# Operand rows of two softmax layers loaded straight from SBUF, eight places per feature, with a reordered opening

## The chip, the cores and the metric

One core of one Trainium2 chip runs the whole kernel. The metric is the device time of one execution in microseconds (us), the median of several runs; lower is better.

## What is computed

Four transformer layers on x of shape 2 x 1024 x 128 (two batches of 1024 tokens, 128 features). Each layer normalises x, shifts and scales it by values made from a small conditioning vector (the modulation), runs an attention and a feed-forward half, and adds each result back through a gate. The change touches the attention halves of layers 0 and 1, and the modulation.

```python
# layer 0: differential attention, 32 score heads of 4 features, 16 value heads of 8
q, k, v = x @ Wq.T, x @ Wk.T, x @ Wv.T          # each 1024 x 128 per batch
w = softmax(q_h @ k_h.T * 4**-0.5)              # full 1024 x 1024 for each head
attn = (w[2i] - lam * w[2i+1]) @ v_i            # then RMS norm per head, @ Wo.T
# layer 1: plain attention, 16 heads of 8 features, with biases and a key mask
w = softmax(q_h @ k_h.T * 8**-0.5 + mask)       # then @ v_h, @ Wo.T + bo
```

Layers 2 and 3 (causal latent attention with experts; linear attention) and the feed-forward halves of all layers are not touched.

## The kernel before

Arrays lie with features on partitions and the 2 x 1024 tokens along the free dimension, in four chunks of 512 tokens (`NC = 4`; chunks 0 and 1 are batch 0). Each stage is a small program for each of the five engines; the engines run their own programs in order and meet at semaphores.

**Opening.** `setup_stage` issues on SP the loads of the conditioning vector, x of batch 0, the identity, x of batch 1 and layer 0's modulation weights; `Norm.on_sp` the loads of the layer's weights. `first_norm` runs the layer norm: `centre(c)` subtracts the mean on PE, ACT squares, `variance(c)` averages on PE, ACT takes Ln and Exp, and DVE's `apply(c)` writes the chunk of `R.h`. The modulation products (12 matmuls of two columns) come after all four chunks on PE, and DVE finishes the modulation (seven short instructions) and then applies chunks 0 to 3.

**Projection** (`project_stage`). For each of eight tiles n (four chunks, query and key) PE projects, ACT rounds the result to bf16 (part 1, L561 or L559), DVE subtracts to get the rest (L608 or L605), ACT rounds that (part 2, L566), DVE subtracts again (part 3, L613). Three bf16 parts carry an f32 operand. SP stores the parts of each chunk to a DRAM tensor `parts_dram`. The value projections go between on PE, and DVE copies them to `A.v` (L627, L624). In layer 0 PE then makes the modulation products of layers 1 to 3 (36 small matmuls, L211).

**Operand rows.** Layer 0 works in 8 pairs of groups, 16 groups of 4 heads; layer 1 in 8 groups. The scores of a head are one bf16 matmul that contracts over 32 rows (layer 0) or 64 rows (layer 1): six products of query and key parts per feature, three rows for the running maximum, in layer 1 one for the mask. `load_rows` fills these rows from DRAM, per head with three transfers for the query and three for the key (L415): 24 transfers for a group of layer 0, 28 for one of layer 1 with the mask. The first group is spread over SP, ACT and POOL. `init_operands` presets the rows on POOL by memsets (L444).

**Softmax** (`softmax_stage`). One unit is a group and half of the queries. First pass: PE makes scores two banks at a time (L836), DVE takes the maximum of each pair (L966), 16 such slots for a unit; DVE joins them, POOL splits the maxima into three bf16 parts (`split`), PE turns them (`turn`, L845), DVE adds them to the query rows (`merge`, L981). Second pass: PE makes scores (L856), ACT takes Exp (L944), PE multiplies by the values (L870). Slots of the first pass of the next unit are put in between by a written order. At the start the 16 slots of unit 0 and some of unit 1 stand alone, with nothing of the second pass beside them.

**Layer 0's end.** DVE combines two maps per chunk (L1016, order 0, 1, 3, 2) with a factor that `lambda_programs` has made in the projection stage; POOL squares them (L815); PE sums the squares (L1078) once all four are there, and only then, in PE's order, comes `last_products`, the last product with the values.

```python
        pe.wait_ge(A.map_squared, 4)
        for c in range(3):
            last = pe.matmul(R.ps[32 * c:32 * c + 32, MS[0], :], W.head_sum[:], sq[:, c, :], ...)
        last.then_inc(ms, 1)
        A.last_products()
```

## Time and profile before

| | us |
|---|---|
| median of 3 runs | 2267.89 (2263.37 to 2268.41) |
| the profiled execution, its own time | 2265.14 |
| its span, first to last instruction | 2263.4 |
| TensorE busy | 2077.2 (92%) |
| VectorE busy | 1595.7 (71%) |
| ScalarE busy | 1358.9 (60%) |
| GpSimd busy | 216.5 (10%) |

The span is laid along a time axis that begins with the first instruction. Layer 0's projection begins at 22.75 us, its first maximum at 48.20 us; layer 1's projection at 742.45 us, its first maximum at 768.43 us. Busy time is an average over stages with different limits, so the windows and the timeline of the stages concerned are read, not the totals. PEclk is the granted TensorE clock as a share of full speed (1.00 is 2.4 GHz, 0.50 is 1.2 GHz).

### The profile page before, as it was taken

What the parts mean: (1) busy time and instruction counts of PE and PEld (TensorE: products, weight loads), DVE (VectorE), ACT (ScalarE), POOL (GpSimd) and SP (SyncE); (2) the same over time, 40 slices, a digit from 0 to 9 for tenths busy, and PEclk for the clock granted to TensorE, in tenths of its full rate; (3) what the DMA queues carried; (4) which work ended last, traced back from release to release, by engine and by line L of the source; (5) the groups of instructions that cost most, each with busy time, mean ns of one, the idle gap of its engine ahead of it and who ended that gap; (6) DMA issues with size and microseconds to landing.
All of it is one profiled execution on the core that took longest, in us unless ns stands there. A gap on an engine that the chain in (4) does not pass through costs nothing. (4 is left out here: it accounts for less than half of the span.)

```text
span 2263.4 us, 40899 instructions
## 1 busy us (share of the span) xinstructions
PE 2077.2 (92%) x15918; PEld 918.9 (41%) x15918; DVE 1595.7 (71%) x2012; ACT 1358.9 (60%) x2699; POOL 216.5 (10%) x397
## 2 busy tenths in 40 slices
PE   5899999999999599999889999999998989999998
PEld 3222222222224222222246566656665434444453
DVE  5999999999964899999455555555555265555553
ACT  3699999999994289999744444444445232222243
POOL 3011111111114301111000000000000010000000
PEclk7799999999999699999999999999999999999999
DMA  4000000000010200010100101010101125555520
GB/s 136 14 16 24 27 22 22 25 26 22 21 28 0 99 16 25 23 40 8 27 4 11 24 14 24 11 23 14 20 10 20 26 61 118 124 118 123 119 63 19
DMA packets 109887, 88.74 MB, mean 39 GB/s; under 512 B 51797, under 2 KB 92629, under 8 KB 105744
## 3 DMA queue, kind: packets, MB, share of 16 engines
q1 hardware_dynamic: 107700, 84.74, 15.4%
q8 instruction: 122, 2.00, 0.4%
q10 hardware_dynamic: 668, 1.04, 0.1%
q0 software_dynamic: 1344, 0.52, 0.1%
q14 instruction: 53, 0.43, 0.1%
HBM read 75.63 MB, written 8.73 MB: 37 GB/s over the span
## 5 line engine op out<-in xcount | busy, mean ns | idle before, releaser
L944 ACT ACTIVATE a0p<-ps 128x512 f32<-128x512 f32 x1024 | 544.3, 599 | 88.2 <-PE ps L856 71.4
L966 DVE TENSOR_REDUCE a0nm<-ps 128x2 f32<-128x1024 f32 x512 | 586.1, 1212 | 12.9 <-PE ps L836 10.7
L870 PE MATMUL ps<-a0p,a0vst 128*32 128x256 f32 x4096 | 328.4, 392 | 27.6 <-ACT a0p L944 14.0
L944 ACT ACTIVATE a1p<-ps 128x512 f32<-128x512 f32 x512 | 275.4, 596 | 58.3 <-PE ps L856 49.8
L966 DVE TENSOR_REDUCE a1nm<-ps 128x2 f32<-128x1024 f32 x256 | 294.5, 1214 | 12.2 <-PE ps L836 11.4
L856 PE MATMUL ps<-a0qm,a0k 32*128 32x512 bf16 x1024 | 276.7, 387 | 0.0
L1783 DVE TENSOR_REDUCE canm<-ps 128x1 f32<-128x128 f32 (+7 forms) x256 | 182.0, 752 | 115.2 <-PE ps L1646 114.6
L1734 ACT ACTIVATE cap_long<-ps,canm 128x1024 f32<-128x1024 f32 (+3 forms) x128 | 121.6, 953 | 190.1 <-DVE canm L1783 190.1
L836 PE MATMUL ps<-a0k,a0q 32*128 32x512 bf16 x1024 | 203.8, 396 | 29.1 <-DVE a0nm L966 21.8
L2015 ACT ACTIVATE ex_s<-ps 128x512 f32<-128x512 f32 x128 | 76.4, 597 | 252.9 <-PE ps L1970 252.9
L836 PE MATMUL ps<-a1k,a1q 64*128 64x512 bf16 x512 | 150.6, 405 | 26.6 <-DMA a1k<-a1mask 14.7
L870 PE MATMUL ps<-a1p,a1vst 128*32 128x256 f32 x2048 | 164.5, 393 | 6.6 <-ACT a1p L944 5.7
L2104 DVE TENSOR_TENSOR ex_su<-ex_s,ps 128x512 f32<-128x512 f32 x128 | 88.0, 688 | 116.2 <-PE ps L1974 115.9
L856 PEld LDWEIGHTS ps<-a0qm,a0k 32*128 32x128 bf16 x1024 | 79.1, 91 | 208.8 <-ACT a0p L944 119.6
L1646 PE MATMUL ps<-cak,caq 64*128 64x512 f32 (+3 forms) x768 | 158.6, 517 | 0.0
L856 PE MATMUL ps<-a1qm,a1k 64*128 64x512 bf16 x512 | 156.8, 386 | 0.0
L1659 PE MATMUL ps<-ident_res,cap_long 128*128 128x128 f32 x832 | 123.2, 281 | 29.1 <-ACT cap_long L1734 18.8
L870 PEld LDWEIGHTS ps<-a0p,a0vst 128*32 128x32 f32 x4096 | 81.6, 108 | 156.0 <-ACT a0p L944 70.7
L1970 PE MATMUL ps<-h_res,f2wg 128*128 128x512 f32 x256 | 130.7, 592 | 0.0
L1974 PE MATMUL ps<-h_res,f2wu 128*128 128x512 f32 x256 | 130.7, 592 | 0.0
L1958 PE MATMUL ps<-ex_hid,f2wd 128*128 128x512 f32 x256 | 130.5, 592 | 0.0
L1659 PEld LDWEIGHTS ps<-ident_res,cap_long 128*128 128x128 f32 x832 | 89.0, 140 | 86.0 <-issue 39.2
(305 smaller groups left out, 2515.1 us busy)
## 6 DMA issues: line engine op xcount, KB each, us to landing
ex_wb<-ex_w_dram SPq DMA_DIRECT2D x62, 512.0 KB, 6.2
carrow<-car_dram SPq DMA_DIRECT2D x32, 256.0 KB, 4.3
xc_res<-a0rec SPq DMA_DIRECT2D x15, 256.0 KB
a0parts<-a0parts_sb SPq DMA_DIRECT2D x8, 384.0 KB, 3.6
a1parts<-a1parts_sb SPq DMA_DIRECT2D x8, 384.0 KB, 3.8
f2wg<-in_ex_gate SPq DMA_DIRECT2D x32, 64.0 KB, 1.8
f2wu<-in_ex_up SPq DMA_DIRECT2D x32, 64.0 KB, 1.9
f2wd<-in_ex_down SPq DMA_DIRECT2D x32, 64.0 KB, 1.9
```

The source lines that it names most:

```text
L836: pe.matmul(R.ps[:, bank + d, :], q[rows, slot, rt, t0:t0 + 128], k[rows, slot, rt, hf * CW:(hf + 1) * CW], start=True, stop=True).then_in ...
L856: pe.matmul(R.ps[:, score_bank(n), :], k[rows, place(u)[3], rt, s * 128:(s + 1) * 128], qm[rows, u % 2, rt, :], start=True, stop=True).the ...
L870: last = pe.matmul(R.ps[32 * j:32 * j + 32, 6, cols], vst[:, g, s, j * HG // 4, :], p[:, s % 2, j, cols], start=(g == 0 and s == 0 and hal ...
L944: act.activation(p[:, s % 2, e, :], R.ps[:, score_bank(n), :], ACT.Exp).then_inc(exp_done, 1)
L966: dve.tensor_reduce(nm[:, u % 2, tb, 2 - 2 * z:4 - 2 * z, hf], R.ps[:, bank:bank + 2, :], X_AXIS, ALU.max, negate=True).then_inc(bank_free, 1)
L1646: last = pe.matmul(R.ps[:, 2 * hh + c, 0:cols], q[rows, hp % 2, b, tb * 128:(tb + 1) * 128], k[rows, hp % 2, b, c * CW:c * CW + cols], sta ...
L1659: last = pe.transpose(R.ps[:, bank, to:to + 128], p[long][:, hh, s * 128:(s + 1) * 128], R.ident[:])
L1734: act.activation(p[long][:, hh, 0:(tb + 1) * 128], src, ACT.Exp, bias=nm[:, a % 4:a % 4 + 1], accum_out=rs[:, b, tb, hh:hh + 1]).then_inc( ...
L1783: dve.tensor_reduce(nm[:, a % 4:a % 4 + 1], src, X_AXIS, ALU.max, negate=True).then_inc(max_done, 1)
L1958: pe.matmul(R.ps[:, i % 4, :], wd[:, (i // 4) % 2, :], hid[:, i % 4, :], start=False, stop=True, skip_group_check=True).then_inc(d_done, 1)
L1970: pe.matmul(R.ps[:, G_BANK + 2 * (i % 2), :], wg[:, slot, :], h_chunk(R, c), start=True, stop=True)\
L1974: pe.matmul(R.ps[:, U_BANK + 2 * (i % 2), :], wu[:, slot, :], h_chunk(R, c), start=True, stop=True)\
```

## The change

Parts stay in SBUF. Every feature has eight rows ("places") in a group's operand tile: place 0 for the mask, 1 to 6 for the six products, 7 of the first three features for the maximum. A transfer takes 16 features of one part of one operand, from 16 neighbouring partitions to 16 partitions at a stride of eight: 12 transfers for a group of layer 0, 24 and 2 for the mask in layer 1. The stores to DRAM are gone. `init_operands` needs fewer memsets.

In the projection only the parts of batch 0 (tiles 0 to 3) are made ahead of the maxima; values and the tiles of chunk 2 are projected too. The tiles of chunk 3 are projected by PE after slots 1 and 3 of unit 0, ACT makes parts 1 and 2 of batch 1, and POOL, not DVE, does the two subtractions (eight instructions of 128x512), ahead of its `split(0)`. The first group's loads are on SP in layer 0, and on SP (query, mask), POOL and ACT (key) in layer 1.

The opening of layer 0 is reordered: identity and x first, the modulation products after the first variance, DVE applies chunks 0 to 2 and, in the projection stage, chunk 3. The modulation of layers 1 to 3 goes from the projection stage into the last unit of layer 0's softmax (six shares on PE, the seven DVE instructions ahead of chunk 3 among the combined maps), with the factor lambda ahead of the maps.

```diff
@@ setup_stage
-    loads = [cT, x[0], ident, x[1], L0_wmod]
+    loads = [ident, x[0], cT, L0_wmod, x[1]]
@@ first_norm
-        for c in range(NC):
-            norm.centre(pe, c)
-            ...
-        modulation[0](pe)
+        norm.centre(pe, 0)
+        norm.centre(pe, 1)
+        pe.wait_ge(R.setup_sems.ones_done, 3)
+        norm.variance(pe, 0)
+        products(pe)
+        norm.centre(pe, 2)
+        norm.variance(pe, 1)
+        norm.variance(pe, 2)
+        pe.wait_ge(step, 1)
+        norm.centre(pe, 3)
+        norm.variance(pe, 3)
@@ load_rows
+PART_OF = ((0, 0, 0, 1, 1, 2), (0, 1, 2, 0, 1, 0))
+    for part in parts:
+        for i in range(6):
+            if PART_OF[operand][i] == part:
+                for rt in range(A.row_tiles):
+                    f = first + rt * rows
+                    queue.dma_start(dst[1 + i:122 + i:8, slot, rt, :], A.parts[f:f + rows, operand, part, b, :])\
+                         .then_inc(loaded or A.ld[slot], 16)
@@ project_stage, on_sp
-        for c in range(NC):
-            ...
-                sp.dma_start(A.parts_dram[o, :, b * C:(b + 1) * C, t].rearrange("s f t -> f s t"),
-                             parts[:, o, :, b, t]).then_inc(stored[b], 16)
+        sp.wait_ge(A.inited[0], A.n_inited[0])
+        for part in range(3):
             for o in range(2):
+                if bias and o == 1:
+                    continue
+                part_waits(sp, part, o)
+                load_rows(A, 0, 0, o, sp, (part,))
@@ project_stage, on_pool and its second parts
+            pool.wait_ge(part3, 4)
             init_operands(A, 1)(pool)
+    def second_parts(pool):
+        for n in range(4, 9):
+            if n < 8:
+                ...
+                pool.wait_ge(part1, n + 1)
+                pool.tensor_tensor(full[:, n - 4, :], full[:, n - 4, :], parts[:, o, 0, b, t], ALU.subtract).then_inc(taken, 1)
+            if n > 4:
+                ...
+                pool.wait_ge(part2, n)
+                pool.tensor_tensor(parts[:, o, 2, b, t], full[:, n - 5, :], parts[:, o, 1, b, t], ALU.subtract).then_inc(third, 1)
@@ project_stage, on_pe
+        first_batch(0)
+        first_batch(1)
+        second_batch(2, 0)
+        second_batch(2, 1)
+        for c in range(NC):
             values(c)
+        A.among_maxima = {1: lambda: second_batch(3, 0), 3: lambda: second_batch(3, 1)}
@@ project_stage, on_act (after the parts of tiles 0 to 3)
+        if bias:
+            act.wait_ge(A.inited[0], A.n_inited[0])
+            for part in (1, 2):
+                part_waits(act, part, 1)
+                load_rows(A, 0, 0, 1, act, (part,))
+        for c in (2, 3):
+            if not bias:
+                copy_values(c)
+            for o in range(2):
+                first_part(2 * c + o)
+        for n in range(4, 8):
+            act.wait_ge(taken, n - 3)
+            second_part(n, full[:, n - 4, :])
@@ project_stage, on_dve (after the parts of tiles 0 to 3)
+        if last_chunk:
+            last_chunk.apply(dve, 3)
+        copy_values(0)
+        copy_values(1)
+        if bias:
+            copy_values(2)
+            copy_values(3)
+            key_mask(1)
@@ softmax_stage, on_pool
-        pool.wait_ge(*A.v_done)
         stage_v(0)
+        A.second_parts(pool)
         split(0)
@@ softmax_stage, on_pe
-        pe.wait_ge(*A.rested)
-        if A.modulated:
-            pe.wait_ge(A.modulated, 1)
         for i in range(16):
+            if i < 2:
+                pe.wait_ge(A.v_done[i], 8)
             p1_slot(0, i)
+            if i in A.among_maxima:
+                A.among_maxima[i]()
...
+                if A.modulation and u == UNITS - 1 and 0 < s < 7:
+                    A.modulation[0](pe, s - 1, 6)
@@ softmax_stage, on_dve
         if A.maps:
+            lambda_programs(W)[2](dve)
             for c, rows in COMBINED:
+                if c == 3:
+                    A.modulation[1](dve)
```

## Rows read from the trace of the kernel before

**Rows 1.** The page, costliest groups: busy, mean ns | idle before, releaser.
```profile
L944 ACT ACTIVATE a0p<-ps 128x512 f32<-128x512 f32 x1024 | 544.3, 599 | 88.2 <-PE ps L856 71.4
L966 DVE TENSOR_REDUCE a0nm<-ps 128x2 f32<-128x1024 f32 x512 | 586.1, 1212 | 12.9 <-PE ps L836 10.7
```

**Rows 2.** Windows: stretch, length, busy us (instructions) of PE, PEld, DVE, ACT, POOL; PEclk, DMA.
```profile
16.60:22.70 6.10, 0.00 (x0) 0.00 (x0) 5.78 (x17) 0.07 (x1) 0.00 (x0) 0.74 0.09 33
...
47.50:72.00 24.50, 12.93 (x49) 2.64 (x49) 23.36 (x23) 0.00 (x0) 4.22 (x11) 0.50 0.12 36
72.00:81.00 9.00, 8.21 (x55) 1.58 (x55) 8.27 (x8) 5.82 (x11) 0.00 (x0) 0.50 0.09 27
81.00:100.00 19.00, 17.60 (x208) 5.51 (x200) 18.82 (x19) 17.51 (x35) 1.26 (x5) 1.00 0.03 7
...
753.00:767.00 14.00, 0.05 (x1) 0.00 (x0) 7.75 (x25) 2.31 (x6) 10.24 (x16) 0.64 0.59 196
```

**Rows 3.** Timeline, layer 0's opening: start, length, engine, line, instruction, count [idle before].
```profile
5.77 0.29 DVE L274 TENSOR_TENSOR centre_res<-centre_res,ident_res 128x128 f32<-128x128 f32 x1 [5.77 <-DMA ident_res<-in_ident]
...
9.48 1.02 PE L307 MATMUL ps<-sq_res,ones_res 128*128 128x512 f32 x2
...
15.12 1.40 PE L211 MATMUL ps<-mod_sil,mod_w 128*128 128x2 f32 x12
...
17.71 0.69 DVE L314 TENSOR_TENSOR xc_res<-rstd_res,ps 128x512 f32<-128x512 f32 x1
...
22.75 3.73 PE L541 MATMUL ps<-h_res,a0w 128*128 128x512 f32 x4 [6.23 <-DVE a0w L578]
...
24.83 0.60 ACT L561 ACTIVATE a0parts_sb<-ps 128x512 bf16<-128x512 f32 x1 [1.68 <-PE ps L541]
```

**Rows 4.** Timeline, from layer 0's parts to its first maxima.
```profile
30.70 0.68 DVE L613 TENSOR_TENSOR a0parts_sb<-rstd_res,a0parts_sb 128x512 bf16<-128x512 f32 x1
...
36.06 4.30 PE L211 MATMUL ps<-mod_sil,mod_w 128*128 128x2 f32 x36 [0.86 <-DVE rstd_res L608]
36.59 4.11 SPq L415 DMA_DIRECT2D a0q<-a0parts  x6
...
37.31 3.25 DVE L627 COPY a0v<-ps 128x128 f32<-128x128 f32 x16
...
41.12 11.80 ACTq L415 DMA_DIRECT2D a0k<-a0parts  x15
...
47.54 0.61 PE L836 MATMUL ps<-a0k,a0q 32*128 32x512 bf16 x4 [7.18 <-DMA a0k<-a0parts]
...
48.20 12.53 DVE L966 TENSOR_REDUCE a0nm<-ps 128x2 f32<-128x1024 f32 x11 [4.07 <-PE ps L836]
```

**Rows 5.** Timeline, the end of layer 0's softmax.
```profile
657.84 2.07 DVE L1016 SCALAR_TENSOR_TENSOR rstd_res<-a0maps,a0cols 128x512 f32<-128x512 f32 x3
657.88 19.11 ACT L944 ACTIVATE a0p<-ps 128x512 f32<-128x512 f32 x36 [0.24 <-PE ps L856]
...
661.38 5.31 SPq L761 DMA_DIRECT2D a0maps<-a0on  x8
...
668.06 0.75 DVE L1016 SCALAR_TENSOR_TENSOR rstd_res<-a0maps,a0cols 128x512 f32<-128x512 f32 x1 [8.16 <-DMA a0maps<-a0on]
...
668.89 1.04 POOL L815 TENSOR_TENSOR sq_res<-rstd_res 128x512 f32<-128x512 f32 x1 [4.54 <-DVE rstd_res L1016]
...
676.26 1.03 PE L1078 MATMUL ps<-sq_res,a0head_sum 128*32 128x512 f32 x6
```

**Rows 6.** One line's instructions (the division on POOL): ns min/median/max, starts.
```profile
L797 POOL TENSOR_TENSOR a0on<-a0o,xc_res x15: 1269/1272/1280, 130.6 to 660.1; 128x512 f32<-128x512 f32 x15
```

**Rows 7.** Timeline, layer 1's opening.
```profile
742.45 1.88 PE L541 MATMUL ps<-h_res,a1w 128*128 128x512 f32 x4
...
750.45 0.68 DVE L613 TENSOR_TENSOR a1parts_sb<-rstd_res,a1parts_sb 128x512 bf16<-128x512 f32 x1
...
768.43 18.19 DVE L966 TENSOR_REDUCE a1nm<-ps 128x2 f32<-128x1024 f32 x16 [5.16 <-PE ps L836]
```

More of the change, by code:

```diff
@@ L157, in __init__ @@
         self.heads_of_group, self.mask = heads_of_group, mask
-        self.parts_dram = nc.dram_tensor(name + "parts", [2, 3, B * C, T], BF16, kind="Internal").ap()
-        self.mask_dram = nc.dram_tensor(name + "mask", [groups, T], BF16, kind="Internal").ap() if mask else None
-        self.first_part = 4 if mask else 3
+        self.spare = (7, 15, 23)
         self.scale = dim ** -0.5
@@ L420, in load_group @@
     load_rows(A, idx, slot, 1, queue)
+    if A.mask:
+        load_mask(A, idx, slot, queue)
 def init_operands(A, stage):
@@ new lines, in on_act, with biased, first_part, second_part @@
+    def on_act(act):
+        def biased(dst, n):
+            src = R.ps[:, n, :]
+            return act.activation(dst, src, ACT.Identity, bias=bqk[:, n % 2:n % 2 + 1]) if bias else act.activation(dst, src, ACT.Copy)
+        def first_part(n):
+            b, t = chunk(n // 2)
+            act.wait_ge(qk, n + 1)
+            if n >= 4:
+                biased(full[:, n - 4, :], n)
+            biased(parts[:, n % 2, 0, b, t], n).then_inc(part1, 1)
+        def second_part(n, left):
+            b, t = chunk(n // 2)
+            act.activation(parts[:, n % 2, 1, b, t], left, ACT.Copy).then_inc(part2, 1)
+        def copy_values(c):
+            act.wait_ge(vp, c + 1)
+            for i in range(4):
+                dst, src, _b = value_rows(c, i)
+                act.activation(dst, src, ACT.Copy).then_inc(v_done[1], 1)
+        if layer == 1:
+            decay_programs(R, W)[0](act)
+        if bias:
+            act.wait_ge(scaled, A.n_scaled)
+        for n in range(5):
+            if n < 4:
+                first_part(n)
+            if n:
+                act.wait_ge(rested, n)
+                second_part(n - 1, rest[:, n - 1, :])
+        if bias:
[11 more added lines that the diff above has]
+            second_part(n, full[:, n - 4, :])
```

291 lines of the change are left out of this document (127 added, 164 removed).

## The prediction, made before the change was run

> **What bounds the kernel now.** I read the page's groups first, then the windows over both openings, then the timeline inside them. In the middle of layer 0 three engines run at nearly the same pace: ACT's 1024 Exp cost 599 ns each and DVE's 512 reductions 1212 ns, each almost without a pause [rows 1], and a window there has DVE busy 18.82 of 19.00 us, PE 17.60 and ACT 17.51 [rows 2]. The change leaves that work alone: as many matmuls over as many rows, as many reductions, as many Exp. What it can move lies where nothing of this overlaps. Layer 0 begins its maxima at 48.20 us, layer 1 at 768.43 us [rows 4, 7]. Ahead of both, PE stands idle, 7.18 us ahead of its first scores in layer 0, for a DMA [rows 4], and in layer 1 PE is busy 0.05 of 14.00 us [rows 2]. So each microsecond by which the last operand row comes earlier shortens the kernel, until the values or the preset rows come last. The third place is the end of layer 0's softmax, where new work is put ahead of a wait.
>
> **Opening of layer 0, up to the parts.** The identity, for which the first centring waits until 5.77 us, is issued ahead of x. When x lands isn't shown; I take 0.5 us, bounds 0 and 0.8. The first variance then ends at 10.0 us (before 9.48 + 1.02) [rows 3]. The products follow at once, 1.40 us, to 11.4. They need the modulation weights, now issued ahead of x of batch 1; in the old order they were there by 15.12 [rows 3], so a wait of up to 3.7 us is possible, and I take none. From the products' end to the first apply it was 17.71 - 16.52 = 1.2 us: chunk 0 applied at 13.9, where the old kernel had it at 19. But PE, in its own order, has two centrings and two variances of 1.0 us (15.4), waits 0.8 for the last square, and ends the last variance at 17.2. So PE gates, not h, and the projection begins at 17.2, not 22.75: 5.5 gained. ACT has Ln and Exp of chunk 3 behind that variance (1.3 us), and makes its first rounding at 18.7, not 24.83: 6.1 gained. From there to tile 3's third part it took 31.38 - 24.83 = 6.55 [rows 3, 4]; DVE's two instructions a tile set that, and they stay: 25.2.
>
> **The loads of the first group.** Removed are the stores (the loads of SP, ACT and POOL began only at 36.59, five microseconds behind the third part) and the old loads, of which PE waited for the last until 47.54 [rows 4]. New are 12 transfers from SBUF to SBUF on SP. The nearest row is the gather of the maps, SBUF to SBUF, eight transfers in 5.31 us, so 0.66 each; DVE could go on at 668.06, 1.4 us behind the last issue [rows 5]. The old query loads on SP took 4.11 / 6 = 0.69; the upper bound is 0.79, as 15 issues on ACT took 11.80 [rows 4]; a lower one isn't needed, as will be seen. The first three can go when tile 2 has its first part, about 21.2. Later ones find their parts made, so SP's issues set the end: 21.2 + 12 x 0.66 = 29.1, landed 30.5. First scores then, first maximum 0.7 later (47.54 to 48.20), at 31.2: 17.0 gained. Is something else later? DVE applies chunk 3 (1.2) and copies eight values of 0.20 (3.25 us for 16) [rows 4]: 28.0. ACT has eight copies (taken as 0.3, between that 0.20 and its rounding of 0.60) and four roundings behind its last second part, 24.1 + 2.4 + 2.4 and some 1.6 of waiting for PE's values: 30.5, level with slot 1. So this cover is thin, and issues at any lower price win 0.5 us at most. The memsets of POOL are fewer and end long before. The later groups on SP are issued by 53 us, group 1 by 37, unit 1 needs it near 49.
>
> **Projections among the maxima.** Two tiles of chunk 3 come between slots. At the start of a maxima phase the clock is 0.50 [rows 2], and a tile costs 3.73 / 2 = 1.87 us at that level [rows 3]. A slot costs DVE 12.53 / 11 = 1.14 us and PE 0.61 [rows 4]. Two slots and a tile take PE 3.1 us, DVE 2.3: 0.8 late each time, twice, 1.6 lost (none if the clock were at 1.00, 3.7 if nothing were hidden). Layer 0's opening: -17.0 + 1.6 = -15.4.
>
> **Subtractions on POOL.** Eight of them, and `split(0)` is queued behind them; for that, PE's turn, DVE's merge and every Exp wait. The nearest row is POOL's division of the same shape, 1.27 us [rows 6], so 10.2 us. The last tile is projected at about 36, rounded at 37.5; the second parts come behind it in ACT's order, so POOL does one or two subtractions early, the rest from 38.2, and ends at 46. The join of unit 0 is at 31.2 + 16 x 1.14 + 1.6 = 51. So I cost them at nothing, with 5 us of cover. The Trainium skill, "SBUF — State Buffer", section "SBUF: two separate sides", says that a DVE instruction with two SBUF inputs and a POOL instruction that reads SBUF lock each other out for their whole length. By that page DVE's reductions, which read PSUM, lock nothing; POOL's division ran at 1269 to 1280 ns beside them, which agrees [rows 6].
>
> **Layer 1's opening.** Its projection begins as before, 742.45, and tile 3's third part was there at 751.13 [rows 7]. The decay's Exp ahead (0.2) and a key mask of 0.7 put it at 752.0. SP has 12 query transfers and two of the mask, from tile 2's first part (747.2): 12 x 0.66 + 2 x 0.3 = 8.5, 755.7, landed 757.1. ACT's six key transfers begin behind tile 3's second part, 751.4 + 4.0, landed 756.8; POOL's six begin at 748.4 and even at 0.79 are earlier. DVE's 16 copies end at 755.3. First maximum 757.8 instead of 768.43: 10.6 gained. The two tiles cost 1.6 here too. Layer 1: -9.0. ACT's issues hold up its roundings of batch 1 by 4 us; POOL ends near 773, the join is at 777.6.
>
> **The end of layer 0.** Here the change adds. The 36 small matmuls lay in PE's idle stretch, 4.30 us [rows 4]. Now they are six shares of 0.72 in the last unit, where ACT runs without a pause, 36 Exp in 19.11 us [rows 5], 2.12 a step. How much PE has to spare in a step no row shows; I take 0.4, so 0.3 lost a share, 1.8 in all (bounds 0 and 4.3). Then a wait: chunk 3's map, third of four, now stands on DVE behind the seven modulation instructions, and these behind the last share. PE starts its last step at about 676.26 - 2.1 = 674.2; with five shares' loss (1.5) and the last share the products end at 676.4; seven instructions, 1.2; two maps at 2.07 / 3 = 0.69, 679.0; POOL's last square, 1.04 [rows 5], 680.1; PE's sum of squares at 680.3, not 676.26. Queued behind it are the last products, ACT's take and the whole chain into the feed-forward. Before, the squares had been done at 669.9, with 6 us of cover; that cover is gone. Cost 4.1 us (bounds 2.3 and 6.6). The lambda instructions, 1.4 us, fall in front of the maps and are hidden.
>
> **Sum.** -15.4 - 9.0 + 4.1 = -20.3. The profiled execution took 2265.1 (span 2263.4 and 1.7 around it), which gives 2244.8; the median of the runs lies 2.8 above that execution, so 2247.6, and I say 2248.
>
> **The rivals.**
> 1. The new transfers are dearer: 0.79 an issue, and a landing 1.6 us later, since many are in flight. 3.2 us in each layer: 2254. For it speaks that 24 transfers of the old kind were held until 47.54; against it, the even 0.66 of the gather.
> 2. POOL comes last. If its subtractions took double, 10.2 more less 5 of cover, 5 us in each layer: 2258. It would show as ACT's first Exp behind `split(0)` by more than before.
> 3. The end of layer 0 costs more: the shares not hidden at all (+2.5), and PE idle for some 3 us ahead of its sum of squares, so that the clock falls to 0.50 there (it fell within an idle stretch of 6.10 us, mean 0.74 [rows 2]) and some 4 us of matmuls take 2 us longer: 2252.
> 4. More is gained: the clock stays at 1.00 through the maxima, as PE idles only 3 us ahead of them. In the slow 9.00 us ACT made 11 Exp, in the fast 19.00 us 35 [rows 2]: 5.6 Exp missing, 3 us a layer, and the 1.6 of the tiles. 2248 - 9 = 2239. Against it: PE is little used in the maxima (12.93 of 24.50 us) and stood at 0.50 throughout.
> 5. Slower than before: the clock. A first pass cut up by waits could leave PE at 1.2 GHz well into the units. A slow microsecond makes 1.22 Exp, a fast one 1.84, so it costs 0.34. The slow stretch now ends at 81 us [rows 2]; to eat 20 us and 4.5 more it must last 73 us longer, both layers together. With 100 us more: 2282. The Trainium skill, "TensorE: Matmul & The Clock Gate", section "Part 1: The HAM clock gate", has the clock follow how busy the array has lately been; by it the units, which are no less dense than before, bring it back as before.
> 6. The change doesn't do what it says: the first maximum is held by what the row copies covered (values, weights of the modulation landing late, x), and both ends eat each other: 2266.
>
> **How the numbers follow.** Forecast 0.58, rival 1 0.12, rival 2 0.08, rival 3 0.10, rival 4 0.06, rival 5 0.03, rival 6 0.03. The forecast's own bounds, 0.5 us less to 1.6 more for each layer's issues, the end between 2.3 and 6.6, make 2244 to 2254. The range takes in rivals 1 to 3 and most of 4: 2238 to 2259. Some 0.2% of the time, 4.5 us, is what a measurement of this kernel can tell from no change. Rivals 1 to 4 are all faster by more than that: 0.94, of which I give 0.02 away for what I have not seen: faster 0.92, within 0.2% 0.04, slower 0.04.
>
> **What would show it.** Right: PE's first projection near 17.2 with the wait for a square in front; L966 first at 31 us, with `a0q<-a0parts_sb` transfers on SP ended two microseconds before and 0.6 to 0.7 apart; in layer 1 ten microseconds from the third part's place to the first maximum gone; two gaps of about 0.8 on DVE in the first slots; PE's sum of squares some 4 us behind where the Exp end, released by POOL. Wrong: a first Exp that waits for POOL; PEclk 0.50 beyond 35 us after the first maximum; a first maximum released by ACT's value copies. The prediction fails if the transfers' price or the clock is not as in these rows, or if the first modulation weights land later than 10 us.

## The result, and the profile after the change

| | before | after |
|---|---|---|
| median of the runs, us | 2266.55 (4 runs, 2263.37 to 2268.41) | 2248.45 (4 runs, 2246.54 to 2253.06) |
| the profiled execution, us | 2265.14 | 2250.09 |
| its span, us | 2263.4 | 2248.3 |
| read from DRAM, MB | 75.63 | 62.98 |
| written to DRAM, MB | 8.73 | 2.42 |

The ratio after to before is 0.9925, 95% interval 0.9904 to 0.9945. The forecast was 2248. The sum behind it was less good than its total: it was made against the profiled execution, where it gave 2244.8, and that execution took 2250.09. The medians are 18.1 us apart, the two profiled executions 15.1. The experiments below find why the profiled one came later than the sum; the rest of the match is luck, as the last part says.

The marks of both kernels, read from the timelines (before in [rows 3 to 5, 7]):

| mark, us | before | after | gained so far |
|---|---|---|---|
| layer 0, first projection | 22.75 | 17.89 | 4.9 |
| layer 0, first maximum | 48.20 | 31.44 | 16.8 |
| layer 0, maxima of unit 0 joined | 66.42 | 50.77 | 15.7 |
| layer 0, first Exp | 72.58 | 56.94 | 15.6 |
| maxima of the last unit joined | 653.89 | 638.68 | 15.2 |
| PE's sum of squares | 676.26 | 672.11 | 4.2 |
| layer 1, first projection | 742.45 | 737.39 | 5.1 |
| layer 1, first maximum | 768.43 | 754.53 | 13.9 |
| layer 1, first Exp | 793.25 | 780.07 | 13.2 |
| end of the span | 2263.4 | 2248.3 | 15.1 |

So both openings gave nearly what was forecast, and 11.0 us of it were lost again in one place, the last unit of layer 0. The steps of that unit are the shares' place: a "share" is six of the 36 small matmul instructions, put behind one step of four Exp. The middle is untouched, as the page's groups say (line engine operation, busy, mean ns | idle before, releaser), with 1214 and 599 ns against the 1212 and 599 of [rows 1]:

```profile
L1025 DVE TENSOR_REDUCE a0nm<-ps 128x2 f32<-128x1024 f32 x512 | 586.4, 1214 | 13.2 <-PE ps L892 11.1
L1003 ACT ACTIVATE a0p<-ps 128x512 f32<-128x512 f32 x1024 | 544.6, 599 | 74.9 <-PE ps L912 58.7
```

Timeline of the changed kernel, layer 0's opening (start, length, engine, line, instruction, count [idle before <- releaser]):

```profile
9.47 1.90 PE L305 MATMUL ps<-sq_res,ones_res 128*128 128x512 f32 x2
...
11.18 1.43 PE L209 MATMUL ps<-mod_sil,mod_w 128*128 128x2 f32 x12
...
17.89 3.60 PE L560 MATMUL ps<-h_res,a0w 128*128 128x512 f32 x8
...
28.24 0.59 SPq L418 DMA_DIRECT2D a0q<-a0parts_sb  x1
28.87 0.59 SPq L418 DMA_DIRECT2D a0k<-a0parts_sb  x1
...
31.00 0.40 PE L892 MATMUL ps<-a0k,a0q 32*128 32x512 bf16 x4 [3.27 <-DMA a0k<-a0parts_sb]
...
31.44 4.62 DVE L1025 TENSOR_REDUCE a0nm<-ps 128x2 f32<-128x1024 f32 x4 [3.08 <-PE ps L892]
...
42.62 2.26 POOL L543 TENSOR_TENSOR a0parts_sb<-rstd_res,a0parts_sb 128x512 bf16<-128x512 f32 x2
...
50.77 0.19 DVE L1031 TENSOR_REDUCE a0m<-a0nm 128x16 f32<-128x32 f32 x1
51.04 0.26 POOL L839 TENSOR_TENSOR a0mt<-a0m,a0zero 128x16 bf16<-128x16 f32 x1 [6.15 <-DVE a0m L1031]
...
56.94 0.60 ACT L1003 ACTIVATE a0p<-ps 128x512 f32<-128x512 f32 x1 [13.52 <-PE ps L912]
```

It answers [rows 3, 4]. PE waits only 3.27 us for a DMA ahead of its first scores, where it waited 7.18, and the last of the twelve transfers is issued at 28.87 + 0.59 = 29.46. POOL's subtractions end at 44.88, and POOL is idle 6.15 us before the join releases it: the cover of the forecast.

Layer 1, which answers [rows 7]:

```profile
737.39 3.60 PE L560 MATMUL ps<-h_res,a1w 128*128 128x512 f32 x8
...
749.69 1.29 SPq L424 DMA_DIRECT2D a1k<-pj1mrow  x2
...
753.87 1.04 PE L892 MATMUL ps<-a1k,a1q 64*128 64x512 bf16 x4 [7.60 <-DMA a1q<-a1parts_sb]
...
754.53 2.35 DVE L1025 TENSOR_REDUCE a1nm<-ps 128x2 f32<-128x1024 f32 x2 [3.42 <-PE ps L892]
...
773.48 0.19 DVE L1031 TENSOR_REDUCE a1m<-a1nm 128x16 f32<-128x32 f32 x1
```

And the place of the loss, the last unit of layer 0 ([rows 5] before), first as windows (stretch, length, busy us (instructions) of PE, PEld, DVE, ACT, POOL; PEclk, DMA share, GB/s), then the timeline:

```profile
645.00:650.00 5.00, 4.90 (x54) 1.92 (x46) 0.22 (x1) 4.37 (x9) 3.34 (x3) 1.00 0.09 18
650.00:655.00 5.00, 5.00 (x48) 2.50 (x44) 0.00 (x0) 3.86 (x8) 0.00 (x0) 1.00 0.44 119
655.00:660.00 5.00, 5.00 (x36) 2.17 (x34) 0.00 (x0) 2.75 (x6) 0.00 (x0) 0.63 0.36 81
660.00:665.00 5.00, 5.00 (x32) 2.07 (x28) 0.00 (x0) 2.57 (x5) 0.00 (x0) 0.50 0.02 3
665.00:670.00 5.00, 5.00 (x32) 2.17 (x34) 2.20 (x9) 2.42 (x5) 0.43 (x1) 0.50 0.00 0
```

```profile
648.49 0.83 PE L209 MATMUL ps<-mod_sil,mod_w 128*128 128x2 f32 x6
...
651.27 0.83 PE L209 MATMUL ps<-mod_sil,mod_w 128*128 128x2 f32 x6
...
652.51 2.06 ACT L1003 ACTIVATE a0p<-ps 128x512 f32<-128x512 f32 x4 [0.72 <-PE ps L912]
...
657.24 1.44 PE L209 MATMUL ps<-mod_sil,mod_w 128*128 128x2 f32 x6
...
659.32 1.09 ACT L1003 ACTIVATE a0p<-ps 128x512 f32<-128x512 f32 x2 [1.96 <-PE ps L912]
...
661.71 1.44 PE L209 MATMUL ps<-mod_sil,mod_w 128*128 128x2 f32 x6
...
666.19 1.44 PE L209 MATMUL ps<-mod_sil,mod_w 128*128 128x2 f32 x6
...
672.11 1.07 PE L1143 MATMUL ps<-sq_res,a0head_sum 128*32 128x512 f32 x3 [1.37 <-POOL sq_res L871]
```

At full clock two shares are 2.78 us apart (648.49, 651.27), and ACT idles 0.72 us in that step; a step without a share took 19.11 / 9 = 2.12 [rows 5]. So 0.66 of a share's 0.83 us is on the path. Then, with PE busy in every microsecond, the granted clock falls to 0.50 (1.2 GHz), and a step takes 4.48 us (661.71 to 666.19). The wait for POOL, which the forecast put at the larger half of its 4.1, is 1.37 us. The kernel before showed how little room there was; PE is busy 19.19 of 20.00 us in the same unit, 0.09 us free in each step of 2.12:

```profile
657.00:677.00 20.00, 19.19 (x194) 5.77 (x190) 3.16 (x5) 19.28 (x38) 5.32 (x5) 1.00 0.26 68
```

### The profile page after: what moved, and what is told of

Read it like the earlier page. It is cut to its first block and busy times, and to the rows that moved or that the text cites. A ratio compares the mean times of both kernels' runs of the same rounds, so it can differ in the third digit from the quotient of the medians.

```text
span 2248.3 us, 40661 instructions
## 1 busy us (share of the span) xinstructions
PE 2083.6 (93%) x15918; PEld 919.8 (41%) x15918; DVE 1581.1 (70%) x1988; ACT 1365.1 (61%) x2715; POOL 204.6 (9%) x382
## 3 DMA queue, kind: packets, MB, share of 16 engines
q1 hardware_dynamic: 106016, 79.55, 15.5%
HBM read 62.98 MB, written 2.42 MB: 29 GB/s over the span
## 5 line engine op out<-in xcount | busy, mean ns | idle before, releaser
L1025 DVE TENSOR_REDUCE a0nm<-ps 128x2 f32<-128x1024 f32 x512 | 586.4, 1214 | 13.2 <-PE ps L892 11.1
L926 PE MATMUL ps<-a0p,a0vst 128*32 128x256 f32 x4096 | 333.7, 397 | 26.9 <-ACT a0p L1003 13.9
L1025 DVE TENSOR_REDUCE a1nm<-ps 128x2 f32<-128x1024 f32 x256 | 294.5, 1215 | 10.4 <-PE ps L892 9.5
L1727 PE MATMUL ps<-ident_res,cap_long 128*128 128x128 f32 x832 | 123.2, 281 | 29.1 <-ACT cap_long L1802 18.8
```

What stands on the lines that cost most here:

```text
L926: last = pe.matmul(R.ps[32 * j:32 * j + 32, 6, cols], vst[:, g, s, j * HG // 4, :], p[:, s % 2, j, cols], start=(g == 0 and s == 0 and hal ...
L1025: dve.tensor_reduce(nm[:, u % 2, tb, 2 - 2 * z:4 - 2 * z, hf], R.ps[:, bank:bank + 2, :], X_AXIS, ALU.max, negate=True).then_inc(bank_free, 1)
L1727: last = pe.transpose(R.ps[:, bank, to:to + 128], p[long][:, hh, s * 128:(s + 1) * 128], R.ident[:])
```

## The experiments

The base of most of them is a kernel with one part of the change undone in another way: the 36 small matmuls of the modulation are again done ahead of the maxima. They ran on three chips, each beside the kernel before on the same chip. A "ratio" is the time over that of the kernel before, and a difference "by the ratios" is the difference of two ratios times 2266 us; each ratio is known to within 0.001 to 0.002, 2 to 4.5 us, so smaller differences rest on the traces alone.

**Early modulation (e1_mod_early).** Two shares ahead of the values of chunk 3, four behind them, in bank 6; DVE copies the bank in the projection stage and does its other six instructions at the start of the last unit.

```diff
@@ project_stage, on_pe
         for c in range(NC):
+            if modulation and c == 3:
+                modulation[0](pe, 0, 6)
+                modulation[0](pe, 1, 6)
             values(c)
+        if modulation:
+            for share in range(2, 6):
+                modulation[0](pe, share, 6)
@@ softmax_stage, on_pe, last unit
-                if A.modulation and u == UNITS - 1 and 0 < s < 7:
-                    A.modulation[0](pe, s - 1, 6)
@@ softmax_stage, on_dve
-                if c == 3:
-                    A.modulation[1](dve)
```

> The changed kernel with the 36 modulation products of layers 1 to 3 made ahead of the first maxima of layer 0 (12 of them ahead of the last chunk's values, 24 behind), DVE's copy of them right behind, its six other instructions at the start of the last unit; nothing of it is left among the last unit's steps. Both theories expect the stretch from the first Exp of the last unit to the sum of squares to return from 29.5 us to the 18.4 us of the kernel before, so some 11 us less there, and at most 1.5 us more ahead of the first maximum (now 31.44 us): about 2238 us, or 10 us under the changed kernel.

Measured 2240.55 (2239.53 to 2241.92), ratio 0.9892 (0.9876 to 0.9909), 7.5 us below the changed kernel by the ratios. The first maximum comes at 32.05, 0.6 later; the last unit keeps its clock, and from the join of its maxima to PE's sum of squares it takes 661.74 - 639.23 = 22.5 us (22.4 before, 33.4 after the change):

```profile
655.00:660.00 5.00, 4.80 (x50) 1.40 (x47) 0.00 (x0) 4.86 (x10) 0.69 (x1) 1.00 0.34 80
660.00:665.00 5.00, 4.30 (x44) 1.64 (x43) 0.00 (x0) 4.20 (x8) 0.00 (x0) 1.00 0.18 33
```

So the late modulation as a whole costs the 11 us of the last unit. Not all of it reaches the end: of 10.4 us at the sum of squares (672.11 against 661.74) 7.8 are left at layer 1's projection (737.39 against 729.58) and 8.6 in the profiled executions' times, since the feed-forward half between them took 2.6 us longer here at a lower clock. Three kernels ask which part of it does: its time on PE, its kind of work, or the wait behind it. Each adds to the early-modulation kernel six pieces of work that nobody reads, in the six steps where the shares stood, and no wait for any other engine.

**Twelve instructions of two columns a step (e2_small_late).** Each f32 matmul is two instructions, so these six matmuls are twice a share (1.50 us at full clock, where a share is three matmuls, 0.83).

> e1 with six matmuls of two columns added after each of steps 1 to 6 of the last unit, written to a bank that nobody reads; neither a DVE wait nor a map depends on them. Clock theory: they leave PE so thinly used that the granted clock falls to 0.50 in the last unit, which takes some 28 us instead of 19, so 7 to 9 us over e1 (about 2246). Time theory (my prediction's term: six shares of 0.72 us of which 0.4 fits into PE's slack): clock at 1.00, 1.8 us over e1 (2240). If instead the wait of the third map made the loss, e2 equals e1 within 2 us and the changed kernel keeps 8 us over it.

Measured 2259.6 (2256.54 to 2260.7), ratio 0.9978 (0.9968 to 0.9989): 19 us more than early modulation, beyond every number of the expectation, with twice the work that it reckoned with. The mean clock is 0.56 in 650 to 655 us and 0.50 from there to 680.

**One dense matmul a step (e3_dense_late)**, 128x512 f32, 1.12 us, longer than a share:

> e1 with one f32 matmul of 128 rows and 512 columns after each of the same six steps in place of six small ones, to the same unread bank: at least as much PE time (1.0 us for its two passes at full clock, against 0.83 for a share), but all of the array busy. Clock theory: PEclk stays at 1.00 and the last unit takes 19.1 + 6 x 0.6 = 23 us at most, so 2 to 4 us over e1 and under e2. Time theory: the same as e2 or more.

Measured 2246.41 (2241.48 to 2247.04), ratio 0.9914 (0.9899 to 0.993). The clock stays at 1.00 throughout, PE is as full as in the others, and join to sum of squares takes 667.11 - 638.94 = 28.2 us, 5.7 more than with early modulation: 0.94 for each 1.12. The clock came as the clock theory says, the time didn't (2 to 4 us expected): PE again hides only 0.18 of each piece.

```diff
@@ last unit, in six steps: e2_small_late (range(6)) and e5_share_late (range(3))
+                    for i in range(3):
+                        pe.matmul(R.ps[:, 3, i * B:(i + 1) * B], R.ones[:], R.h[:, 0, 4 + i * B:4 + (i + 1) * B], ...)
@@ e3_dense_late
+                    pe.matmul(R.ps[:, 3, :], R.ones[:], h_chunk(R, 0), start=True, stop=True)
```

**The size of a share (e5_share_late)**, the same with three matmuls:

> The kernel with early modulation, with six matmuls of two columns that nobody reads (the work of three f32 products, six instructions) put into each of six steps of layer 0's last unit: the load on PE of the six shares of the change, without any wait of DVE or POOL behind it. Clock theory: such thin matmuls make the granted clock fall to 0.50 within this unit, as after the change (656 to 680 us); the unit then costs 7 to 9 us more than with early modulation, about 2249. Time theory (a share costs its own 0.72 us at full clock and the clock stays): 6 x 0.72 = 4.3, 2245. Hidden theory of the prediction (0.3 a share): 1.8, 2242.5.

Measured 2251.24 (2248.49 to 2254.65), ratio 0.9939 (0.9926 to 0.9953), 10.6 us above early modulation by the ratios, a little more than the 7 to 9 of the clock theory; the others fall. Windows of this kernel, then of the one with the longer, dense matmul:

```profile
645.00:650.00 5.00, 4.80 (x49) 1.94 (x48) 3.95 (x5) 4.29 (x9) 4.65 (x4) 1.00 0.06 11
650.00:655.00 5.00, 5.00 (x42) 2.07 (x44) 0.75 (x1) 3.28 (x7) 1.35 (x2) 0.71 0.39 102
655.00:660.00 5.00, 5.00 (x34) 1.97 (x26) 0.00 (x0) 2.70 (x6) 0.53 (x1) 0.50 0.34 75
```

```profile
650.00:655.00 5.00, 5.00 (x43) 1.46 (x41) 0.75 (x1) 3.68 (x8) 1.33 (x2) 1.00 0.43 115
655.00:660.00 5.00, 5.00 (x35) 1.41 (x35) 0.00 (x0) 2.98 (x6) 0.40 (x1) 1.00 0.38 71
```

PE's busy time is 5.00 of 5.00 us in both. The thin work lets the clock fall and the dense work doesn't; busy time on the page doesn't tell them apart. Whether it is the few columns or the many weight loads for them (PEld is busy 1.97 to 2.07 of 5.00 us in the one, 1.41 to 1.46 in the other), these kernels don't separate. That all 11 us come back without any wait behind them (673.52 - 639.10 = 34.4) shows that the wait isn't needed to explain the loss.

**The wait alone (e7_dve_late).** The changed kernel with DVE's seven modulation instructions behind all four maps.

```diff
@@ softmax_stage, on_dve
             for c, rows in COMBINED:
-                if c == 3:
-                    A.modulation[1](dve)
...
+            A.modulation[1](dve)
```

> The changed kernel with one thing altered: DVE's seven modulation instructions stand behind all four combined maps, not ahead of chunk 3's, so that no square waits for the modulation. The six shares on PE stay. If the 10 us lost at the end of layer 0 are in the shares and the clock they let fall, only POOL's wait goes, about 1.4 us: 2247. If the wait behind the modulation is what costs (the step of the prediction: 4.1 us less 1.5 to 1.8 for the shares), 2.5 us or more go, 2246 or less, and the clock is back at 1.00 earlier.

Measured 2252.79 (2243.85 to 2254.54), ratio 0.994 (0.9925 to 0.9954). Neither number came: the executions lie in two groups, 2243.85 and 2245.40 with mean granted clocks of 0.979, and 2252.48 to 2254.54 with 0.972 to 0.974. The profiled one is of the first group. Its clock stays at 1.00 through 660 us, with the same six shares in place, and join to sum of squares takes 27.3 us, 4.8 above early modulation:

```profile
655.00:660.00 5.00, 5.00 (x49) 2.13 (x48) 0.00 (x0) 3.59 (x8) 0.35 (x1) 1.00 0.40 82
660.00:665.00 5.00, 5.00 (x47) 2.38 (x44) 1.04 (x7) 3.47 (x8) 0.00 (x0) 0.87 0.03 6
```

So the fall is not certain; it happens in some executions and at different places. Between the two groups lie some 8 us. Its lower group (two executions) lies 0 to 3 us below the lowest four of the changed kernel (2245.38 to 2246.80), which the 1.37 us of the wait would fit, but its upper group (2252.48 to 2254.54) lies where the changed kernel's does (2252.38 to 2254.24). That taking the wait away wins anything in the changed kernel isn't shown.

**The changed kernel once more (e12_change_again).**

> The changed kernel itself, a second time. The clock theory: its executions differ by whether the granted clock falls within layer 0's last unit, and where. The first four took 2246.5, 2246.8, 2250.1 and 2253.1 with mean clocks of 0.978, 0.978, 0.975 and 0.973. If that is the reason, the new ones lie along the same line, 2244 to 2254, the lower ones with the higher mean clock, and the profiled one shows its last unit (first Exp to sum of squares) between 24 us (clock kept) and 30 us. If time and clock aren't linked, the theory falls.

Measured 2250.93 (2245.38 to 2254.24), ratio 0.9925 (0.9909 to 0.9941). All ten executions of the changed kernel, by time, with the mean granted clock: 2245.38, 2246.54, 2246.64, 2246.80 (0.978); 2249.47, 2250.09 (0.975); 2252.38 (0.974); 2253.06, 2253.25, 2254.24 (0.973). They lie on one line. From 0.978 to 0.973 is 0.005 x 2248 = 11 us of full-speed work undone, or 22 us more at half clock, for 7 us of time: 0.32 for each microsecond at half clock, where the forecast had worked out 0.34 from [rows 2]. (The clocks are given to 0.001, so 0.32 is known to a fifth or so.) The line says that the clock makes the spread, not where in the kernel. The kernel before, which has no share in its last unit, spreads as widely: on the chip of this series, 2262.21 to 2269.76 in eleven executions at 0.975 to 0.971. What places a part of it in the last unit is the pair of profiled executions: 2.3 us apart in the last unit (33.4, 35.7) and 2.3 in the whole. The profiled execution of this series belongs to the upper end (span 2250.6): its last unit falls already before 655 us, and from join to sum of squares it takes 673.59 - 637.93 = 35.7 us, which as 31.7 from its first Exp is a little beyond the 30 expected.

```profile
650.00:655.00 5.00, 5.00 (x39) 2.21 (x38) 0.00 (x0) 3.23 (x7) 0.00 (x0) 0.65 0.43 120
655.00:660.00 5.00, 5.00 (x30) 2.49 (x29) 0.00 (x0) 2.17 (x4) 0.00 (x0) 0.50 0.35 76
```

**The opening of layer 0 alone (e4_old_opening, e9_old_opening).** The first is the changed kernel, the second the best kernel below, each with the old order of loads and of the first norm.

```diff
@@ setup_stage
-    loads = [ident, x[0], cT, L0_wmod, x[1]]
+    loads = [cT, x[0], ident, x[1], L0_wmod]
@@ first_norm, on_pe
+        for c in range(NC):
+            norm.centre(pe, c)
+            ...
+        norm.variance(pe, NC - 1)
+        products(pe)
```

> The changed kernel with the opening put back alone: old order of the first loads, all four centrings and variances ahead of the 12 modulation products. DVE still applies chunk 3 behind the parts. Expected by the working of the prediction: first projection at 22.2 to 22.7 us instead of 17.9, first maximum 4.5 to 6 us later than 31.44, the whole 4.5 to 6 us over the changed kernel (2253 to 2254). Rival: SP's loads and ACT's copies take the time up and it costs under 2 us.

Measured 2256.15 (2251.65 to 2259.33), ratio 0.9963 (0.9948 to 0.9977), first maximum 36.72 against 31.44: the 5.3 us of the expectation. The median came 2 us above the range that was expected. The first projection began at 21.00, not at 22.2 or later, so only 3.1 of the 5.3 us were there from the start. The other 2.2 came on the way to the maximum, and what differs there is the clock: ahead of the projection PE sat idle for 2.72 us, and the granted clock was 0.50 from 21 to 25 us, where the changed kernel, which hardly waits there, has 1.00 from 17 to 23. Six instructions of the projection took 5.41 us here, eight of them 3.60 in the changed kernel.

The end of layer 0 in its profiled execution says as much as the opening. The same six shares stand in the last unit, and the clock stays at 1.00 through all of them. Then PE sits idle for POOL, and there the clock falls:

```profile
662.00:668.00 6.00, 6.00 (x59) 3.10 (x57) 0.00 (x0) 4.57 (x9) 0.00 (x0) 1.00 0.20 38
668.00:674.00 6.00, 3.54 (x31) 1.25 (x34) 2.35 (x9) 2.10 (x5) 2.48 (x2) 0.78 0.00 0
674.00:680.00 6.00, 6.00 (x24) 2.24 (x19) 0.75 (x1) 2.60 (x5) 0.00 (x0) 0.65 0.00 0
```

```profile
672.81 1.07 PE L1141 MATMUL ps<-sq_res,a0head_sum 128*32 128x512 f32 x3 [2.46 <-POOL sq_res L869]
```

From join to sum of squares it takes 672.81 - 643.77 = 29.0 us, 6.7 more than before the change: six times 0.66 and the wait of 2.46. That is what the late modulation costs while the clock is kept, and the profiled execution therefore took only 1.6 us more than that of the changed kernel (2251.65 against 2250.09), 5.3 us later at the first maximum or not.

> The kernel with early modulation, moved queues and layer 1's tiles ahead, with the opening of the old kernel: x and the conditioning vector first, identity after them, all centrings and variances ahead of the modulation products. The prediction puts the new opening at 5.5 us (PE) to 6.1 us (first rounding); the changed kernel with this one edit had its first maximum 5.3 us later (36.72 against 31.44). If that is passed on whole, 2235.4 + 5.3 = 2240.7. If part of it is hidden by something else that is late in this kernel, less.

Measured 2242.14 (2240.08 to 2242.39), ratio 0.9888 (0.9873 to 0.9904), 6.75 above its base by the medians and 5.0 by the ratios, with the first maximum 5.7 later (37.23 against 31.52), the last unit's join 5.9 and the start of layer 1's projection 7.4 (the clock in the feed-forward half, which is touched by neither, was lower in this execution). Some 0.9 of the 5.7 is the first variance, which took 1.92 us here and 1.02 in the base, and e4_old_opening and the changed kernel (1.91 and 1.90) don't differ in that. So the new order is worth about 5 us at the first maximum, a little under the forecast's 5.5 to 6.1.

**The issues of the first group (e6_queues).** Early modulation, and in layer 0 the key transfers on POOL; in layer 1 the mask and the third query part on POOL.

```diff
@@ project_stage, on_sp
-                if bias and o == 1:
+                if o == 1 or bias and part == 2:
                     continue
@@ project_stage, on_pool
+            load_mask(A, 0, 0, pool, A.pool_ld)          # layer 1
+            load_rows(A, 0, 0, 0, pool, (2,), A.pool_ld)
...
+            for part in range(3):                        # layer 0
+                load_rows(A, 0, 0, 1, pool, (part,), A.pool_ld)
```

> The kernel with early modulation, with part of SP's first loads moved: in layer 0 the six key transfers of the first group are issued by POOL, in layer 1 the mask and the third query part. If SP's issues set the first scores, as the prediction says: in layer 0 0.8 us earlier (then the values' copies or ACT's keep the bank), in layer 1 two mask issues of 0.65 and two of 0.7, 1.3 to 2.6 us earlier; 2237 to 2238.5. If the landing or PE's projection of values sets them: no change, 2240.5.

Measured 2237.59 (2234.88 to 2242.3), ratio 0.9884 (0.9869 to 0.9899). The number came, but it is 1.8 us below early modulation by the ratios, within what they can tell, and not wholly for the reason. Layer 1's first maximum comes 739.75 - 724.22 = 15.5 us after its projection, against 745.88 - 729.58 = 16.3: 0.8, less than the 1.3 to 2.6. In layer 0 nothing came earlier (13.8 against 14.1 from projection to first maximum): with the issues gone from SP, PE's values and the modulation copy come last. The rest is the clock again: from the last sum of squares of layer 0's attention (671.06; 670.76) to layer 1's projection it took 53.2 us here and 58.8 in the profiled execution of early modulation, whose clock was 0.71 and 0.84 in 680 to 700 us.

**Everything ahead (e8_all_ahead).** As before, and layer 1's tiles of chunk 3 projected ahead of the maxima, where PE waits for a transfer anyway.

```diff
@@ project_stage, on_pe
+        if bias:
+            second_batch(3, 0)
+            second_batch(3, 1)
+            A.among_maxima = {}
```

> Early modulation, the moved queues of the first loads, and in layer 1 the two tiles of chunk 3 projected ahead of the maxima instead of among them. If tiles among the maxima cost DVE 0.7 us in layer 1 and PE has room for them ahead (it waits there for the last transfer), this is 0.7 us below the kernel with the moved queues alone: 2236.5 to 2238. If PE has no such room, since the loads now come earlier, the same or up to 1 us more.

Measured 2235.39 (2234.46 to 2235.75), ratio 0.9866 (0.9852 to 0.9881): the lowest of this study, 13 us below the changed kernel by the ratios; its lead over e6_queues (4 us by the ratios) is not clear of the noise. The 16 maxima of layer 1 now run without a gap, 758.31 - 740.15 = 18.2 us from first to join. With the tiles among them they took 18.5 in e6_queues and 19.0 in the changed kernel, so this edit alone wins 0.3 in the traces, not the 0.7 expected. The four executions lie within 1.3 us, those of e6_queues within 7.4.

**Twice the work on POOL (e10_pool_doubled).** Ten more subtractions behind the eight.

```diff
@@ second_parts, then
+        for n in range(10):
+            pool.wait_ge(third, 4 + n)
+            pool.tensor_tensor(full[:, n % 3, :], full[:, 3, :], parts[:, 0, 0, 0, 0:CW], ALU.subtract).then_inc(third, 1)
```

> The kernel with early modulation, moved queues and layer 1's tiles ahead, with ten more subtractions of 128x512 on POOL behind the eight, results that nobody reads: 10 x 1.15 = 11.5 us in each of the two layers. POOL stood idle 6.15 us ahead of its first split in layer 0 and 9.6 us in layer 1. Cover theory (the prediction's): 5.4 us later in layer 0, 1.9 in layer 1, 2235.4 + 7.3 = 2242.7. If POOL's work isn't hidden at all: 2235.4 + 23 = 2258. If it slows DVE's reductions (1.14 a slot), more than 7.3 and longer reductions.

Measured 2242.74 (2239.55 to 2245.22), ratio 0.9894 (0.9877 to 0.9911): the cover theory's number. POOL's chain becomes the bound, and PE and DVE wait for it:

```profile
44.72 12.22 POOL L557 TENSOR_TENSOR rstd_res<-rstd_res,a0parts_sb 128x512 f32<-128x512 f32 x10
...
56.90 0.26 POOL L870 TENSOR_TENSOR a0mt<-a0m,a0zero 128x16 bf16<-128x16 f32 x1
...
58.51 0.61 PE L932 MATMUL ps<-identb_res,a0mt 128*128 128x128 bf16 x4 [4.87 <-POOL a0mt L878]
```

From join to first Exp it took 10.2 us in layer 0 and 7.3 in layer 1, against 6.2 and 6.6: 4.0 and 0.7 lost, less than 5.4 and 1.9, since PE has four slots of unit 1 to do there before it needs POOL. The cover was thus near 8 us, not 6. First maximum to join is 19.33 us with and without the added work: DVE's reductions aren't slowed by POOL at all. The medians lie 7.35 apart, the profiled executions 6.5, the ratios 6.3; what goes beyond 4.7 I don't explain, so that the number agrees with the cover theory better than the trace does.

**A clock kept up through the maxima (e11_dense_among).** The best kernel with dense bf16 matmuls that nobody reads: two behind each lone slot, eight among the modulation shares, sixteen ahead of layer 1's scores.

```diff
+        def dense(n):
+            for _ in range(n):
+                pe.matmul(R.ps[:, 4, :], parts[:, 0, 0, 0, 0:128], parts[:, 0, 0, 0, 0:CW], start=True, stop=True)
...
+        pe.wait_ge(part1, 5)
```

> The kernel with early modulation, moved queues and layer 1's tiles ahead, with bf16 matmuls of 128x512 that nobody reads: two behind each of the slots that stand alone, two ahead of each of four modulation shares, and sixteen ahead of layer 1's first scores. The clock now falls to 0.50 at the first maxima and comes back only some 34 us later in layer 0, 30 in layer 1. If dense work keeps it at 1.00 there: the first Exp of unit 0 run at full clock, 3 us a layer by the prediction's fourth rival, 2228 to 2232. If it doesn't, two fillers (0.86 at half clock) and the slot's 0.61 overrun DVE's 1.14 by 0.33 in each of some 16 slots, 5 us a layer: 2240 to 2246.

Measured 2242.99 (2239.68 to 2245.22), ratio 0.9894 (0.9879 to 0.9909). Windows with the filler, then without:

```profile
31.00:45.00 14.00, 12.81 (x61) 4.35 (x60) 11.94 (x12) 4.56 (x9) 7.80 (x8) 1.00 0.23 53
45.00:56.00 11.00, 8.28 (x39) 2.04 (x38) 10.97 (x11) 0.00 (x0) 2.39 (x7) 1.00 0.11 26
56.00:60.00 4.00, 2.42 (x13) 0.50 (x13) 3.81 (x5) 1.86 (x4) 0.00 (x0) 0.83 0.00 0
60.00:64.00 4.00, 3.90 (x32) 0.83 (x35) 3.67 (x4) 2.59 (x5) 0.00 (x0) 0.50 0.02 4
```

```profile
31.00:45.00 14.00, 9.73 (x28) 1.93 (x24) 12.71 (x12) 4.56 (x9) 7.48 (x7) 0.50 0.23 53
45.00:56.00 11.00, 5.82 (x24) 1.35 (x24) 10.86 (x12) 0.00 (x0) 1.63 (x6) 0.50 0.09 20
56.00:60.00 4.00, 3.21 (x16) 0.56 (x14) 3.70 (x4) 2.26 (x5) 0.00 (x0) 0.50 0.00 0
60.00:64.00 4.00, 4.00 (x35) 0.82 (x32) 3.61 (x4) 2.53 (x6) 0.00 (x0) 0.54 0.00 0
```

The filler does what it should: 1.00 through all the maxima. But it gains next to nothing, and the time lies in the range that was expected for a clock that does not stay. DVE sets the pace there, with 1.14 us a slot at either clock; the gap of the tiles goes (18.2 us instead of 19.3 from first maximum to join), and 0.4 from join to first Exp. And where the Exp begin and the filler stops, the clock falls after all, between 58 and 59 us (0.83 in that microsecond), and is back at about 65, without the filler at 64. So if the clock has a price here, it is in the first ten microseconds of the units, which the filler didn't reach. The 7.6 us more are for the most part an error of the experiment: the wait for ACT's fifth part, which the filler needs, stands in layer 1 behind ACT's six issues and held PE for 4.52 us; projection to first maximum there took 748.28 - 726.83 = 21.5 us against 15.5. Whether filler in the first steps of the units would pay wasn't tried.

## Why the prediction was right, and where not

- **Opening of layer 0.** Projection forecast 17.2, came 17.89; first rounding 18.7, came 19.35; third part of tile 3 25.2, came 25.23 (5.88 behind the first rounding where I took over the old 6.55, which had been measured with PE at 0.50 in its first 3.6 us); last issue 29.1, came 29.46; first maximum 31.2, came 31.44. The 0.7 at the start is in the first variance, which ran 1.90 us instead of 1.02 and put the products at 11.18 instead of 10.0. That is the pace of half the clock, but the profile gives 1.00 there, so why it was slow stays open; in e8_all_ahead it took 1.02, and the projection began at 16.85. The modulation weights were in time. Rival 6 is out, and rival 1 too in this layer: issues of 0.59 to 0.63, landed 1.5 us behind the last.
- **Tiles among the maxima.** Forecast 1.6 lost, lost 19.33 - 18.22 = 1.1 in layer 0 and 0.7 in layer 1 (18.95 against 18.22). The mechanism is right, the overlap a little better. e11_dense_among takes it away in layer 0 and wins the 1.1 between first maximum and join; e8_all_ahead takes it away in layer 1, where by then 0.3 was left of it.
- **POOL.** Forecast end 46 with 5 us of cover; end 44.88 with 6.15 idle; 1.15 for a subtraction, not 1.27. e10_pool_doubled confirms that it was hidden: 12.2 us more on POOL cost 4.0 in layer 0, so rival 2 needed nearly twice the work.
- **Layer 1.** Forecast 10.6 to the first maximum, came (768.43 - 742.45) - (754.53 - 737.39) = 8.8. The mis-sized term is SP's: 0.74 for a query transfer instead of 0.66, and 0.65 for a mask transfer where I had put 0.3 with no row behind it. e6_queues moves four issues away and wins 0.8. To the first Exp: forecast 9.0, came 8.1.
- **The end of layer 0.** Forecast 4.1 lost, lost 11.0: the step that failed. "I take 0.4, so 0.3 lost a share" had no row, though one was to be had: PE had 0.09 free in a step. A share took 0.83 us, not 0.72, and 0.17 of it was hidden, so a share cost 0.66 (4.0 in all, within the bound of 4.3 that I kept). The other 2.6 of the 4.1, the wait for POOL's last square, was 1.37, since the last shares delayed PE itself and the wait ran beside that; with the clock kept it was 2.46 (e4_old_opening). With both sizes put right, the sum at full clock is 4.0 + 2.46 = 6.4, near my upper bound of 6.6, and e4_old_opening measured 6.7. The remaining 4 us are the clock, which I left out of the forecast and put into rival 3 with an idle stretch ahead of the sum of squares as its cause. In both profiled executions of the changed kernel it fell earlier, with PE busy without a pause, on thin matmuls. From share to share the steps then lose 0.66, 0.66, 1.07, 2.35 and 2.36, together 7.1; the other 3.9 lie between the last share and the sum of squares, the wait of 1.37 among them. Rival 3 as I wrote it did happen in e4_old_opening, where the clock kept up through the shares and fell when PE idled.
- **Rival 4**, a clock at 1.00 through the maxima: it was 0.50, and e11_dense_among shows that 1.00 there would have given 1.1 us to the join and 1.55 to the first Exp of layer 0, not 4.6 a layer. The 3 us a layer that I worked out from the missing Exp would lie in the first steps of the units; no run here had the full clock there.
- **The median.** My sum missed the profiled execution by 5.3 us, and the forecast missed the median by 0.4. Between the two lies luck. I had added 2.8 because the median lay that far above the profiled execution before the change; after it the median lay 1.6 below, and these 4.4 us made good most of the 5.3. The executions differ by their mean clocks (e12_change_again), and which one is profiled has nothing to do with the mechanism. A second series gave 2250.93. The 1.9 us gained between layer 1's first Exp and the end I haven't followed.

## What to carry to other kernels

Where a stage runs with one engine's pace and another nearly as full, price an insertion at its whole duration unless a row shows the gap that takes it: 0.83 us inserted cost 0.66. Small matmuls of two columns are cheap in a stretch where PE waits anyway (36 of them cost 0.6 us there, in e1_mod_early) and dear inside a dense one: six shares with the wait behind them cost 6.7 us with the clock kept and 11 where it fell. And if a kernel's executions spread by 9 us, compare their mean granted clocks first: here they put ten executions of one kernel on one line. The line is that kernel's own. With filler the mean clock was 0.991 and the time still 2243, because the clock was raised where PE sets no pace.

## What the hardware showed that was not expected

- The granted clock fell to 0.50 while PE was busy in 5.00 of 5.00 us, on six f32 instructions of two columns in each step of some 2.8 us; a dense 128x512 f32 matmul of 1.12 us in the same place left it at 1.00.
- Whether and where it falls differs between executions of the same work: at 656 us and at 651 us in two profiled executions of the changed kernel, not before 663 in one of e7_dve_late with the same six shares, and in one of e4_old_opening only when PE had nothing to do, at 671 us. The Trainium skill, "TensorE: Matmul & The Clock Gate", section "Part 1: The HAM clock gate", ties the clock to how busy PE has lately been; that PE was busy in 5.00 of 5.00 us where the clock fell (e5_share_late) shows that the busy time of the profile isn't what can be read for it.
- The feed-forward half between the layers, which no kernel here changed, ran at a clock anywhere between 0.67 (e3_dense_late, 690 to 700 us) and 1.00 in stretches of ten microseconds, and took between 53.2 us (e6_queues) and 58.8 us (e1_mod_early).
- Transfers of 16 rows from SBUF to SBUF were issued on SP at 0.59 to 0.63 us in layer 0 and 0.74 in layer 1 (beside the issues of ACT at 0.63 and POOL at 0.49), those of a mask row at 0.65.
- POOL's 128x512 subtractions (1.15 us) and DVE's reductions out of PSUM (1.14 a slot) ran beside each other from 44.7 us to the join at 50.5 in e10_pool_doubled, without slowing the reductions (19.33 us from first maximum to join either way).
